# Cross-attention and mixture layers on one core: sums, key rotations and running maxima in smaller pieces placed along the program

## The reference

```python
x = x + L0_xattn(layernorm(x), ctx, ...)
x = x + L0_ffn(layernorm(x), ...)
x = x + L1_xattn(layernorm(x), ctx, ...)
x = x + L1_ffn(layernorm(x), ...)

# xattn: 16 heads, head size 128, rotated queries (192, layer 0 only) and keys (64)
q_big = einsum('bshk,hkq->bshq', (x @ Wq.T), w_kc_q)      # layer 0: then rotated
kv_r  = kv_c * cos + rotate_half(kv_c) * sin              # "rope" of the context
q_r = einsum('bshq,hqr->bhsr', q_big, W_qr)
k_r = einsum('bld,hdr->bhlr', kv_r, W_kr)
attn = softmax(q_r @ k_r.T)                               # over 1500 context rows
ctx_c = einsum('bhsl,bld->bhsd', attn, kv_r)
out = (ctx_c through w_kc_kv, all heads) @ Wo.T
```

## Time and profile before

| | |
|---|---|
| median of 3 runs | 3785.76 us (3784.65 to 3798.95) |
| profiled execution | 3784.75 us, span 3783.0 us |
| TensorE busy | 3122.5 us, 83% |
| VectorE busy | 2096.5 us, 55% |
| GpSimd busy | 1654.5 us, 44% |
| ScalarE busy | 1261.1 us, 33% |
| mean granted TensorE clock | 0.888 of full |

### The profile page before, as it was taken

How to read it: one execution, slowest core, us unless ns; L and a number is a source line. 1 busy time by engine, 2 the same in 40 slices (tenths; PEclk the granted TensorE clock), 3 DMA queues, 4 the chain that set the end, 5 groups by cost and what they waited for, 6 DMA issues and landing times. The chain is left out here.

```text
span 3783.0 us, 43017 instructions
## 1 busy us (share of the span) xinstructions
PE 3122.5 (83%) x16008; PEld 1727.9 (46%) x16008; DVE 2096.5 (55%) x2343; ACT 1261.1 (33%) x1747; POOL 1654.5 (44%) x952
## 2 busy tenths in 40 slices
PE   7678988788887789887888768986998789877997
PEld 6434446444474344553444534453444444454445
DVE  3566656666466665666665545454554455445545
ACT  3123333133341334332333323422343234322442
POOL 0445534555435455244653235611662156414651
PEclk9789989898988899888999879987998899888998
DMA  6323203132112322132220232113221312122310
GB/s 230 113 53 79 53 33 102 45 79 57 47 55 76 76 64 46 53 92 57 64 68 31 71 89 70 35 44 78 67 51 46 78 47 69 49 49 52 80 56 10
DMA packets 117803, 247.48 MB, mean 65 GB/s; under 512 B 30416, under 2 KB 82880, under 8 KB 110039
## 3 DMA queue, kind: packets, MB, share of 16 engines
q1 hardware_dynamic: 117590, 244.57, 24.5%
HBM read 171.24 MB, written 48.27 MB: 58 GB/s over the span
## 5 line engine op out<-in xcount | busy, mean ns | idle before, releaser
L1317 DVE TENSOR_REDUCE maxpart<-pair 112x2 f32<-112x1000 f32 x768 | 920.4, 1198 | 739.8 <-PE pair L840 739.8
L1204 POOL TENSOR_TENSOR sums<-sums,prob 125x896 f32<-125x896 f32 x472 | 1016.5, 2154 | 305.1 <-ACT prob L1091 259.5
L1091 ACT ACTIVATE prob<-wide 125x896 f32<-125x896 f32 x768 | 704.3, 917 | 941.1 <-PE wide L866 931.6
L881 PE MATMUL single<-prob,kv 125*64 125x448 f32 x3072 | 772.4, 582 | 0.9
L840 PE MATMUL pair<-kparts,qhigh 64*112 64x500 f32 x1536 | 403.4, 522 | 286.5 <-DVE maxpart L1317 264.1
L840 PEld LDWEIGHTS pair<-kparts,qhigh 64*112 64x112 f32 x1536 | 143.3, 183 | 820.7 <-DVE maxpart L1317 595.9
L861 PE MATMUL wide<-qhigh,kparts 64*125 64x448 f32 x3072 | 491.0, 399 | 0.0
L1204 POOL TENSOR_TENSOR sums<-prob 125x896 f32<-125x896 f32 x64 | 133.8, 2091 | 623.8 <-ACT prob L1091 623.8
L861 PEld LDWEIGHTS wide<-qhigh,kparts 64*125 64x125 f32 x3072 | 278.4, 193 | 160.2 <-issue 130.4
L866 PE MATMUL wide<-shift,ones_row 64*125 64x448 f32 x1536 | 296.7, 382 | 44.0 <-DMA shift<-maxrow 44.0
L861 PE MATMUL wide<-qlow,kparts 64*125 64x448 f32 x1536 | 295.5, 380 | 0.0
(11 more groups left out here) (314 smaller groups left out, 4250.0 us busy)
## 6 DMA issues: line engine op xcount, KB each, us to landing
kparts<-keys_merged SPq DMA_DIRECT2D x64, 750.0 KB, 9.1
wexp_low_values<-in_experts SPq DMA_DIRECT2D x68, 384.0 KB, 3.1
kparts<-kparts SPq DMA_DIRECT2D x96, 250.0 KB, 3.1
keys_merged<-kparts SPq DMA_DIRECT2D x32, 750.0 KB, 8.6
recip<-zrec_merged SPq DMA_DIRECT2D x112, 112.0 KB, 2.8
raw<-in_ctx SPq DMA_DIRECT2D x33, 375.0 KB
w_low_values<-w_merged SPq DMA_DIRECT2D x64, 192.0 KB, 2.4
values_merged<-kv SPq DMA_DIRECT2D x32, 375.0 KB
```

Source lines behind the costliest of these rows:

```text
L881: mm = pe.matmul(mix_acc[64 * half:64 * half + DC, 0:HQ], kv[:, j % 3, t, :], prob[:, (j * LT + t) % NPROB, half * HQ:(half + 1) * HQ], st ...
L1091: nc.scalar.activation(prob[:, n_ % NPROB, :].rearrange("p (a b) -> p a b", a=2), acc[0:LP, :, 0:HQ], ACT.Exp)\
L1204: nc.gpsimd.tensor_tensor(dst, first_in, prob[:, n_ % NPROB, :], ALU.add).then_inc(s["pool_sum"], 1)
L1317: V.tensor_reduce(maxpart[:, j % 2, t:NMAX:4, b], acc[0:TQ, :, 0:LB], AX.X, ALU.max).then_inc(*R.signal_drained(kind, *key))
```

## The change

- The sums: `POOL_TILES` goes from 10 to 11. GpSimd adds tiles 0 to 10; VectorE has one addition left per sequence, of tile 11 and GpSimd's sum, at `context`. The last sequence of a pass keeps its split.
- The rotations: `rope` becomes two `ropecos` and two `rope`, each of six tiles instead of twelve, at t = 1, 2, 3 and 4. `rope_done` now counts to two per sequence. In the head of layer 0, the rotation and transposition of sequence 1 move from its end to heads 6 to 11.
- The maxima: in the head of the pass they no longer stand in bunches of three but one by one between the queries, the last ones in three PSUM regions by turns (`PAIR`, 0 and 1). The first four of sequence 1 come before `maxT` of sequence 0. In the loop, `keyT`, `norm` and `maxT` now stand ahead of the `smax` of their tile.
- The transfers: the stores of keys and values are a step of their own, `stash`, at t = 9 behind the transfers of `shift`; the load of the next raw context stands behind the third `keyT`; `spread` is at t = 8 and `share` at t = 10; `fetch` of layer 1 is at t = 2.

```diff
-POOL_TILES, POOL_LAST = 10, 5
+POOL_TILES, POOL_LAST = 11, 5
...
-    def maximum(j, n):
-        add("smax", j, n % 4, n // 4, region=PAIR)
-    def last_maxima(j):
-        for c in range(3):
-            add("smax", j, 3, c, region=PAIR)
+    def maximum(j, n, region=PAIR):
+        add("smax", j, n % 4, n // 4, region=region)
+    def rope(j, parts=(0, 1)):
+        for part in parts:
+            add("ropecos", j, part)
+        for part in parts:
+            add("rope", j, part)
...
+        rope(0)
         for c in range(3):
-            keys(0, c)
-        for n in range(H + 2):
-            if n == H - 3:
-                add("rotate", 1)
-            if n == H:
-                add("rope", 1)
+            add("keyT", 0, c, region=3 + c)
+        for n in range(H + 1):
             if n + SPLIT_AHEAD < H:
                 add("wsplit", n + SPLIT_AHEAD)
             if n < H:
                 add("qwide", n, region=n % 2)
             if n >= 3 and n % 2:
                 add("query", (n - 3) // 2, region=2)
-            if n >= 7 and n % 4 == 3 and n < H:
-                for c in range(3):
-                    add("smax", 0, n // 4 - 1, c, region=PAIR)
+            if n >= 6 and (n - 6) % 4 < 3:
+                add("smax", 0, (n - 6) // 4, (n - 6) % 4, region=PAIR)
+            if n == 6:
+                add("stash", 0)
+                add("rotate", 1)
+            if n == 7:
+                rope(1)
+            if 9 <= n < 12:
+                keys(1, n - 9)
+            if n == 12:
+                add("stash", 1)
+        for i in range(3):
+            maximum(1, i, (0, 1, PAIR)[i])
+        add("query", NPAIR - 1, region=2)
+        for c in range(3):
+            add("smax", 0, 3, c, region=(0, 1, PAIR)[c])
     else:
         for p in range(NPAIR):
             if p < 2:
@@ -109,19 +118,17 @@
             if p + SPLIT_AHEAD < NPAIR:
                 add("wsplit", p + SPLIT_AHEAD)
             add("query", p, region=p % 3)
-            if p >= 3 and p % 2:
-                for c in range(3):
-                    add("smax", 0, p // 2 - 1, c, region=PAIR)
-    last_maxima(0)
+            if p >= 4:
+                add("smax", 0, (p - 4) // 3, (p - 4) % 3, region=PAIR)
+        for n in range(4, 9):
+            add("smax", 0, n // 3, n % 3, region=(PAIR, 0, 1)[n % 3])
+        for c in range(3):
+            add("smax", 0, 3, c, region=(PAIR, 0, 1)[c])
+        for i in range(3):
+            maximum(1, i, (PAIR, 0, 1)[i])
     add("maxneg", 0)
-    if layer == 0:
-        keys(1, 0)
+    maximum(1, 3)
     add("maxT", 0, region=3)
-    if layer == 0:
-        keys(1, 1)
-        keys(1, 2)
-    for n in range(EARLY_MAX):
-        maximum(1, n)
     last = None
     for j in range(BG):
 
@@ -129,7 +136,7 @@
             ahead = (j + 1, t + EARLY_MAX) if t + EARLY_MAX < LT else (j + 2, t + EARLY_MAX - LT)
             if layer == 0 and t == 0 and j + 2 < BG:
                 add("rotate", j + 2)
-            if layer == 1 and t == 1 and 2 < j + 2 < BG:
+            if layer == 1 and t == 2 and 2 < j + 2 < BG:
                 add("fetch", j + 2)
             add("score", j, t, region=t % 2)
             if j + 1 < BG and t == 8:
@@ -138,21 +145,25 @@
                 add("mix", *last)
                 if last[1] == LT - 1:
                     add("context", last[0])
-            if ahead[0] < BG:
-                maximum(*ahead)
             last = (j, t)
             if t == 1 and j:
                 add("norm", j - 1, region=3)
+            if j + 1 < BG and t == 9:
+                add("maxT", j + 1, region=3)
             if layer == 0 and t in (5, 6, 7) and j + 2 < BG:
                 keys(j + 2, t - 5)
-            if t == 3 and j:
+            if layer == 0 and t == 9 and j + 2 < BG:
+                add("stash", j + 2)
+            if ahead[0] < BG:
+                maximum(*ahead)
+            if t == 8 and j:
                 add("spread", j - 1)
-            if t == SHARE_AT[2] and j:
+            if t == 10 and j:
                 add("share", j - 1, 2)
-            if j + 1 < BG and t == 9:
-                add("maxT", j + 1, region=3)
-            if layer == 0 and t == 3 and j + 2 < BG:
-                add("rope", j + 2)
+            if layer == 0 and t in (1, 2) and j + 2 < BG:
+                add("ropecos", j + 2, t - 1)
+            if layer == 0 and t in (3, 4) and j + 2 < BG:
+                add("rope", j + 2, t - 3)
...
+                    if kind == "stash":
+                        j, = key
+                        sp.wait_ge(s["rope_done"], 2 * (j + 1))
                         sp.dma_start(scratch["values"][BG * g + j], kv[:, j % 3, :, :].rearrange("p t d -> p (t d)"))\
                             .then_inc(s[f"values_moved_{j % 3}"], 16)
                         for b in range(3):
                             sp.wait_ge(*R.drained("keyT", j, b))
                         sp.dma_start(scratch["keys"][BG * g + j], kparts[0:DC, j % 3, :, :].rearrange("p a l -> p (a l)").bitcast(F32))\
                             .then_inc(s[f"keys_moved_{j % 3}"], 16)
-                    if kind == "rope" and key[0] + 2 <= BG:
+                    if kind == "keyT" and key[1] == 2 and key[0] + 2 <= BG:
...
+                    if kind == "ropecos":
+                        j, part = key
+                        tiles = slice(part * LT // 2, (part + 1) * LT // 2)
                         if j:
                             dve.wait_ge(s[f"ctx_loaded_{j}"], 16)
-                            dve.wait_ge(s["rope_done"], j)
-                        V.tensor_tensor(rope_c[:], r, c["cosk"][:], ALU.mult).then_inc(s["rope_cos"], 1)
-                        dve.wait_ge(s["rope_cos"], j + 1)
+                            dve.wait_ge(s["rope_done"], 2 * j)
+                        V.tensor_tensor(rope_c[:, tiles, :], raw[:, j % 2, tiles, :], c["cosk"][:, tiles, :], ALU.mult).then_inc(s["rope_cos"], 1)
+                    elif kind == "rope":
+                        j, part = key
+                        tiles = slice(part * LT // 2, (part + 1) * LT // 2)
+                        dve.wait_ge(s["rope_cos"], 2 * j + part + 1)
                         dve.wait_ge(s["rope_sin"], 2 * (j + 1))
                         if j >= 3:
 
                             dve.wait_ge(s["premix"], LT * (j - 2))
                             dve.wait_ge(s[f"values_moved_{j % 3}"], 16 * (j // 3))
-                        V.tensor_tensor(kv[:, j % 3, :, :], rope_c[:], rope_s[:], ALU.add).then_inc(s["rope_done"], 1)
+                        V.tensor_tensor(kv[:, j % 3, tiles, :], rope_c[:, tiles, :], rope_s[:, tiles, :], ALU.add).then_inc(s["rope_done"], 1)
...
-                        dve.wait_ge(s["dve_sum"], vector_sums(j + 1) - 1)
+                        other = sum_dve
+                        if vector_sums(j + 1) - vector_sums(j) == 1:
+                            dve.wait_ge(*R.drained("score", j, LT - 1))
+                            if j:
+                                dve.wait_ge(*R.filled("norm", j - 1))
+                            other = prob[:, (j * LT + LT - 1) % NPROB, :]
+                        else:
+                            dve.wait_ge(s["dve_sum"], vector_sums(j + 1) - 1)
                         dve.wait_ge(s["pool_sum"], pool_sums(j) + pool_tiles(j) - 1)
-                        V.tensor_tensor(sum_dve, sum_dve, sum_pool[:, j % 2, :], ALU.add).then_inc(s["dve_sum"], 1)
+                        V.tensor_tensor(sum_dve, other, sum_pool[:, j % 2, :], ALU.add).then_inc(s["dve_sum"], 1)
```

26 lines of the change are left out of this document (9 added, 17 removed).

## The result

The changed kernel takes 3445.06 us, median of 4 runs (3442.93 to 3446.14), against 3785.95 us (3784.65 to 3798.95) for the kernel before on the same chip: a ratio of 0.909 (95% interval 0.907 to 0.911). Predicted were 3453 us. The profiled execution took 3445.47 us, its span is 3443.7.

A forecast was written before the change was run, and what follows sets the result against it. The loops were taken as bound by TensorE, with its gaps and clock to win; in the heads it idles partly. Terms 150 + 68 + 68 + 46 = 332 us off 3784.75 gave 3453 us, range 3395 to 3590.

The forecast's parts named there:

- loop of layer 0: Attention loop of layer 0: 17.0 + 11.0 us of waits and 20 of clock, less 10.5 left, 37.5 per pass, 150 in four.
- loop of layer 1: Attention loop of layer 1: 15 us of waits and 3 of clock, less 1 left, 17 per pass, 68 in four.
- head of layer 0: Head of layer 0: 21 us of waits less 9 new, less 2, plus 7 of clock, 17 per pass, 68 in four.
- head of layer 1: Head of layer 1: maxima from 31 to 16.4 us, less 2 for `shift` and 1 for splits, 11.5 per pass, 46 in four.
- the step on `shift`: Layer 0 loop: with the store of keys behind, the 1.85 us wait goes; `shift` lands some 0.5 us before it is needed.
- Rotations: Layer 0 loop: four pieces over four tiles replace the 2.83 us wait plus 1.85 for `shift`; 1.75 us per sequence left.
- the rival that the lock gave: Layer 0 loop: smaller pieces no cheaper each, up to 4 x 2.15 us waiting per sequence; about 6 x 1 us less won.
- the sentence on `share`: Layer 1 loop: `share` waits at most half a microsecond for the spread inverse, with 0.9 us in hand on TensorE.
- the rival "`shift` is late": `shift` late behind `spread` on SP: 207 us in both layers, total 3660; layer 0 alone 3540; together chance 0.12.
- The clock: Both loops: granted clock 0.97 or more; 20 us per pass regained in layer 0, 3 in layer 1.
- the rival in which the clock doesn't come back: Layer 0: the wait left at t = 5 costs one clock fall per sequence, 41 us, and a few in heads; 3500, chance 0.2.
- GpSimd's share of the sums: Per sequence: 21.5 us of GpSimd additions fit in 27, cost nothing; without that cover up to 2.15 us on `norm`.

## Why the prediction was right

The sum was 332 us, measured were 339. Its terms:

| | predicted | measured |
|---|---|---|
| loop of layer 0 | -150 | -120 |
| loop of layer 1 | -68 | -57 |
| head of layer 0 | -68 | -91 |
| head of layer 1 | -46 | -68 |

So the total came out this close by luck: the loops gained 41 us less and the heads 45 more, for the most part for unrelated reasons. The mechanisms held but for the step on `shift`, in the sizes below.

- **Rotations.** Right in the waits. TensorE waits 1.18 us for the last piece (1.1 predicted), and some 0.4 for a maximum behind `keyT` (0.4). Not right in the pieces: `kv` was to last 0.5 to 2.5 us, unequal, and all 48 halves last 1.30 to 1.35. That smaller pieces aren't cheaper, the rival that the lock gave, is true in its price (25.8 us against 16.0) and false in what it did to the maxima, since each piece stood in a tile with room. I used the rule for the pieces and didn't draw the conclusion from it: with two whole ones in two places the wait for `kv` goes altogether, and the kernel is 50 us faster.
- **`shift` in layer 0.** This step failed: "`shift` lands some 0.5 us before it is needed". It lands 1.46 to 1.95 us late, four times per loop. I took 3 us from the inverse until SyncE is free; with the raw context ahead SyncE waits 3.8 us for the store alone, and `shift` is issued 5.2 us behind the inverse. The same delay broke the sentence on `share`, which was to wait at most half a microsecond: it waits 2.8 to 3.3 us at these four places. It is the layer 0 half of the rival "`shift` is late", which I priced at 87 us (3540); four waits per loop and the clock that mostly stayed made it 42 in the run with the raw context behind. With those, the loop's gain is 162, against the 150 of the sum.
- **The clock.** Predicted 0.97 or more in both loops; measured 0.98 in the first three passes of layer 0 and 0.97 to 0.98 in layer 1, but 0.95 in the fourth pass of layer 0. I had priced each late `shift` with 1.7 us of clock. The tiles show where it was paid: the tile t = 1 behind a late `shift` takes 2.88 us where the granted clock stays at 1.00, and 3.25 to 5.37 where it falls (0.68 to 0.81 over t = 0 and 1). Two such tiles of the second pass, clock in the third column from the end:

```profile
762.90:765.80 2.90, 2.90 (x22) 1.34 (x20) 1.72 (x2) 1.24 (x3) 0.90 (x1) 1.00 1.01 252
794.80:799.20 4.40, 4.40 (x20) 2.01 (x18) 1.75 (x2) 1.13 (x3) 1.64 (x1) 0.61 0.91 227
```

  It fell at 7 of the 16 late `shift`: at one in each of the first three passes, at all four in the last. With two whole rotations, where the wait for `kv` is gone and `shift` is as late as before, it fell at 1 of 16; with the maximum ahead of `keyT` at all 16. So the rival in which the clock doesn't come back fell as it was put, a fall at t = 5 in each sequence; but the clock did fall 7 times behind the waits for `shift`.
- **Loop of layer 1.** `packed_recip` waits for nothing, as predicted. The missing 11 us are the first `shift`, for which I had 2 us in the head's sum; it waits 2.8 to 4.9 in the loop, 16.5 us in four passes, behind two fetches. Moving one of them gave 13 us.
- **GpSimd's share of the sums.** I costed it at nothing and named it as the cure of the wait of 1.22 us. It is worth nothing or a few us of loss; two additions in a row do no harm in the new order. The sign of being wrong that I named, `sums` on VectorE released by GpSimd, came once in the second pass of each layer (2.1 us), late in the loop, where no maxima stand behind it.
- **Heads.** The mechanism was right, the size too small. In layer 1 the waits for maxima fell from 17.0 to 5.3 us per pass (two PSUM regions and `pair` together); I had counted a maximum with 1.20 us, and they follow each other every 1.10. The busy time of TensorE fell by 3.5 us besides, at a clock of 0.73 instead of 0.62, for which I had nothing. In layer 0 TensorE's busy time fell by the 7 us of my clock term (76.14 to 69.13), and the rest of the head by 16 us instead of 10: I had 9 us of new waits, and those for the maximum are 5.1. The `shift` that I charged to it, 2.1 us, stands in the loop with 1.3.

## What to carry to other kernels

Place first, then size: a long operation on a shared engine belongs between two urgent ones that leave it room. Cutting it up didn't pay here, since each piece that meets the other engine's long operation waits for its end anew: two whole ones in two places beat four halves in four by 50 us. In a single queue, a small transfer that something waits for (and above all a store that is read back) can be as slow as the bulk that was issued ahead of it; put the bulk behind, and look at each edit of the order together with the others, since here one undone alone cost its loop more than all of them together had gained. When a wait goes away, compare the lengths of the steps and not the recorded waits: with the maximum ahead of `keyT` 0.75 us of waits left the list per sequence, and the steps got 0.25 us shorter. And when a total comes true, compare its terms: here two errors of over 40 us stood against each other.

## What the runs showed of the hardware

- A VectorE addition or product of 125 x 384 with both inputs in SBUF takes 0.55 us when GpSimd is idle and 1.07 to 1.35 when it starts during one of its additions; with four in one place the average is 1.6 (`rope_c` 1.82, `kv` 1.48). One that starts during an addition ends 0.41 to 0.42 us after it, one of 125 x 768 0.81 to 0.82 after it.
- Reductions of 1000 columns that take 1.20 us each follow each other every 1.10 us when the next one's input is ready: 3.32 us for three.
- The same waits don't always cost the same clock. Four waits for `shift` of 1.60 to 1.95 us stand in the second pass of layer 0 at 0.98 (one fall), four of 1.69 to 1.76 in the fourth at 0.95 (four falls), a loop of 252.7 us instead of 246.8. In the kernel before, waits of 1.62 to 1.93 for `shift` stood between longer ones of 2.8, and the loop was at 0.92. What decides between the cases isn't shown.
- The two transfers of 56 x 8 numbers behind 1.9 MB were through 13.1 us after the issue of the bulk, whether they were themselves issued 3.2 or 5.1 us behind it.
- A store of 3.5 KB takes 1.4 us until the next issue may follow in layer 1 with nothing large ahead (2464.21 to 2465.59 in the run with the transfers' times as before), 2.0 in layer 0 behind the copies of keys alone, 3.8 behind 375 KB, 9.5 behind 1.5 MB.
